# Expert products of eleven groups in three fp16 passes, an earlier load of the next tokens, and one lower half of E on the Pool engine

## The reference

```
x: (2, 2048, 256)            two sequences b, 2048 tokens, 256 channels, float32
x = x + layernorm(attention(layernorm(x)))          linear attention, no softmax
h = layernorm(x)
logits[b,m,n,p] = sum_d h[b,m,d] * phi[d,n,p]       n: 64 experts, p: 32 slots each
dispatch = softmax over b of logits                 2 sequences: a tanh of the difference
combine  = softmax over (n,p) of logits
slots[b,n,p,:] = sum_m h[b,m,:] * dispatch[b,m,n,p]
y[b,n,p,:] = slots[b,n,p,:] @ W[n] + bias[n]        W[n]: 256 x 256
out[b,m,:] = sum_{n,p} y[b,n,p,:] * combine[b,m,n,p]
x = x + layernorm(out)
```

## Time and profile before

| | us |
|---|---|
| median of 3 runs (654.32 to 654.46) | 654.41 |
| the profiled execution, whole | 654.63 |
| its span in the trace | 652.4 |
| PE busy | 630.5 (97%) |
| DVE busy | 437.7 (67%) |
| ACT busy | 367.3 (56%) |
| POOL busy | 237.5 (36%) |
| fp32 expert products in the block stage, L1606, PE busy | 23.2 |

### The profile page before, as it was taken

The page is one execution under the profiler, slowest core; times in us unless marked ns, Lnnn a source line. Parts: engine busy times, 40 slices in busy tenths (PEclk is TensorE's granted clock), DMA queues, the critical chain, the costliest instruction groups (busy, mean ns, idle before and its releaser), DMA issues.

```text
span 652.4 us, 15309 instructions
## 1 busy us (share of the span) xinstructions
PE 630.5 (97%) x5353; PEld 395.8 (61%) x5353; DVE 437.7 (67%) x859; ACT 367.3 (56%) x712; POOL 237.5 (36%) x416
## 2 busy tenths in 40 slices
PE   8999999999999999999999987799999999999996
PEld 7898645445444444444444455577777777777775
DVE  4978898733333423234333588999999988888885
ACT  5666876742333323324345295777777777777773
POOL 5365887710000000000000052555555555555555
PEclk9999999999999999999999999999999999999999
DMA  8910032325544544454455521132222222222201
GB/s 270 400 61 1 9 70 49 66 61 154 137 133 127 137 133 128 133 133 118 104 161 132 155 74 65 41 127 92 91 92 90 89 88 88 88 88 88 88 16 34
DMA packets 70167, 68.72 MB, mean 105 GB/s; under 512 B 6258, under 2 KB 66675, under 8 KB 67827
## 3 DMA queue, kind: packets, MB, share of 16 engines
q1 hardware_dynamic: 67792, 66.09, 34.4%
q10 hardware_dynamic: 2338, 2.16, 0.9%
HBM read 43.32 MB, written 23.07 MB: 102 GB/s over the span
## 4 chain that ended last, share of the span: by engine, by line
PE 75%; DVE 10%; POOL 5%; ACT 5%; issue 4%; DMA 1%; POOLq 0%; SPq 0%; DVEq 0%; ACTq 0%
PE psL L1589 23%; PE psM L1576 11%; PE psL L1708 10%; PE psM L1726 7%; PE psM L1727 6%; PE psM L1730 6%; PE psM L1606 3%; POOL small L489 2%; PE psL L1474 2%; ACT r_xn L868 1%; DVE small L1278 1%; DVE r_xn L1297 1%; ACT r L868 1%; DMA xres<-in_x 1%; PE psM L1532 1%
## 5 line engine op out<-in xcount | busy, mean ns | idle before, releaser
L1589 PE MATMUL psL<-r,r_xn 128*128 128x512 f16 x768 | 176.4, 379 | 0.8 <-DVE r L1119 0.8
L1589 PEld LDWEIGHTS psL<-r,r_xn 128*128 128x128 f16 x768 | 73.3, 98 | 91.6 <-issue 6.8
L1117 DVE TENSOR_SCALAR r<-r 128x512 f16<-128x512 f32 x64 | 29.0, 453 | 96.3 <-ACT r L758 96.3
L1576 PE MATMUL psM<-phs,xx 128*128 128x512 f16 (+1 forms) x384 | 93.2, 379 | 0.0
L758 ACT ACTIVATE r<-psM,small 128x512 f32<-128x512 f32 x64 | 43.6, 682 | 75.9 <-PE psM L1576 75.1
L576 POOL MEMSET r_xn<- 128x16 f16 x1 | 0.2, 173 | 234.9 <-PE psL L1589 234.9
L1708 PE MATMUL psL<-phs,r 128*32 128x512 f16 x1344 | 75.1, 379 | 2.0 <-DMA r<-xx 1.5
L1576 PEld LDWEIGHTS psM<-phs,xx 128*128 128x128 f16 x384 | 37.3, 98 | 44.8 <-issue 0.7
L868 ACT ACTIVATE r<-psL,small 128x512 f32<-128x512 f32 x60 | 41.9, 776 | 31.3 <-DVE small L1305 22.0
L489 POOL TENSOR_TENSOR small<-small,epst 128x2 f32<-128x2 f32 (+3 forms) x75 | 56.9, 759 | 6.2
L1708 PEld LDWEIGHTS psL<-phs,r 128*32 128x32 f16 x1344 | 34.6, 97 | 38.3 <-issue 2.6
(11 more groups left out here) (208 smaller groups left out, 1292.7 us busy)
## 6 DMA issues: line engine op xcount, KB each, us to landing
logit_difference<-r SPq DMA_DIRECT2D x256, 64.0 KB, 1.8
xx<-logit_difference SPq DMA_DIRECT2D x16, 1024.0 KB, 5.2
r<-in_ffn_w SPq DMA_DIRECT2D x15, 1024.0 KB, 5.5
out<-r SPq DMA_DIRECT2D x32, 128.0 KB, 1.7
xres<-in_x SPq DMA_DIRECT2D x7, 512.0 KB, 11.0
r<-in_phi SPq DMA_DIRECT2D x1, 2048.0 KB, 18.1
expert_bias<-r ACTq DMA_DIRECT2D x1, 2048.0 KB, 20.0
r<-expert_bias SPq DMA_DIRECT2D x16, 128.0 KB, 2.2
```

The source lines that it names most:

```text
L1576: ins = mm(bk[j % 2][:, :].rearrange("p (q m) -> p q m", q=EP), xxT[:, 1, j, hx, k, :], phw[:, hp, k, :, bass.ds(nb, 1), :].rearrange("p q ...
L1589: ins = mm(psL[:, i * 512:(i + 1) * 512], x3n[:, b, j, hx, k * P:(k + 1) * P], thl[:, j % 2, hs, :], start=(j == 0 and hx + hs == 0), stop ...
```

## The change

- The products of groups 0 to 10 (all of blocks 1 and 2, three of block 3) go in three fp16 passes. ACT writes the high half of a block's slots (`split_slots_hi`, at j = 0) and of a group's scaled weights (`weight_hi`, at j = 1, 4, 8, 12), DVE the low halves (`split_slots_lo` at j = 1, `weight_lo` at j = 2, 5, 9, 13). DVE finds a power of two for the weights of a group: `weight_top` (j = 2, 6, 10, 14) reads all 2048 columns, `weight_scale16` (j = 3, 7, 11, 15) brings the maximum over partitions in 15 small instructions. The bias instruction undoes the scale.
- The product moves one tile later on PE: behind j = 2, 6, 10, 14 (13 in the last block); bias and `y_sum` move to j = 3, 7, 11, 15 (14 in the last block).
- The weight halves (`Wp`) lie in r_3, so the load of `Wx` moves into block 3; SP's loads of `Wt` wait for `W_split` and not for the product.
- `load_x1` of the combination loop no longer waits for the mask, so `load_d` is first behind it.
- `lo(0, 1, 0)` is made by POOL.

```
-                    if j % 4 == 2:
-                        sp.wait_ge(yp_done, (nb - 1) * TB + (q + 1))
+                    if j % 4 == 0:
+                        sp.wait_ge(y_out, (nb - 1) * TB + (q + 2))
+                        sp.dma_start(by[:, (q + 1) % 2], ...)
+                    if j % 4 == 2 and not (last and q == TB - 1):
+                        sp.wait_ge(W_split, (nb - 1) * TB + (q + 1))
                         sp.dma_start(Wt[:, q % 2], ...)
...
             def loads(j):
+                wait_apart(sp, l_done, 4 * j)
+                load_x1(j)
                 wait_apart(sp, m0_masked, j)
-                load_x1(j)
                 load_d(j)
...
             mean(1, 0)
+            pool.wait_ge(eh_ready[0], 3)
+            nc.gpsimd.tensor_tensor(eT0[:, 1, 0:8, :]..., ET0[:, 0:1024],
+                                    eT0[:, 0, 0:8, :]..., ALU.subtract).then_inc(el0_pool, 1)
             lo_second(1)
...
+            def split_slots_hi(nb):
+                act.wait_ge(slots_evac, nb * 4 + 4)
+                act.wait_ge(yp_done, (nb - 1) * TB)
+                copy(slots_half[0]..., slT...).then_inc(slots_hi, 1)
+            def weight_hi(nb, q):
+                act.wait_ge(W_scaled, (nb - 1) * TB + (q + 1))
+                act.wait_ge(yp_done, (nb - 1) * TB + q)
+                copy(Wp[:, 0]..., Wt[:, q % 2]..., scale=sW[:, q % 2:q % 2 + 1]).then_inc(W_hi, 1)
             def block_act(nb, last):
                 for j in range(NJ):
                     tanh(nb, j)
                     d_copy(nb, j)
-                    if j % 4 == 2:
+                    if j == 0:
+                        split_slots_hi(nb)
+                    if j in (1, 4, 8) or j == 12 and not last:
+                        weight_hi(nb, j // 4)
+                    if j in (3, 7, 11, 14 if last else 15):
                         y_sum(...)
...
+            def weight_top(nb, q):
+                dve.wait_ge(W_loaded[w], ...)
+                own.add(V.tensor_reduce(wmax, Wt[:, w]..., AX_X, ALU.max, apply_absolute_value=True))
+            def weight_scale16(w):
+                # each line below waits for the one before it
+                transpose(topT, wmax.broadcast_to([P, Q]))
+                tensor_reduce(wquad, topT, AX_X, ALU.max)
+                4 x tensor_copy(wgath[0:Q, q:q + 1], wquad[q * Q:(q + 1) * Q])
+                tensor_reduce(wtop[0:Q, 0:1], wgath[0:Q], AX_X, ALU.max)
+                4 x tensor_copy(wtop[q * Q:(q + 1) * Q, 1:2], wtop[0:Q, 0:1])
+                tensor_scalar(max 2^-100); tensor_scalar(and exponent); tensor_scalar(* 2^-13); reciprocal
+            def split_slots_lo(nb):
+                dve.wait_ge(slots_hi, nb)
+                V.tensor_tensor(slots_half[1]..., slT..., slots_half[0]..., ALU.subtract).then_inc(slots_lo, 1)
+            def weight_lo(nb, q):
+                dve.wait_ge(W_hi, (nb - 1) * TB + (q + 1))
+                V.scalar_tensor_tensor(Wp[:, 1]..., Wt[:, q % 2]..., sW[...], Wp[:, 0]...,
+                                       ALU.mult, ALU.subtract).then_inc(W_split, 1)
             def block_dve(nb, last):
                 for j in range(1, NJ):
                     split(nb, j)
-                    if j % 4 == 2:
-                        y_bias(...)
+                    if j == 1:
+                        split_slots_lo(nb)
+                    if j in (2, 5, 9) or j == 13 and not last:
+                        weight_lo(nb, q)
+                    if j % 4 == 2 and not (last and q >= 2):
+                        weight_top(nb + (q + 1) // TB, (q + 1) % TB)
+                    if j in (3, 7, 11, 14 if last else 15):
+                        y_bias(..., not (last and q == TB - 1))
+                        if not (last and q >= 2):
+                            weight_scale16((q + 1) % 2)
...
+                    pe.wait_ge(W_split, yb_ * TB + (q + 1))
+                    if q == 0:
+                        pe.wait_ge(slots_lo, yb_ + 1)
+                    for b in range(B):
+                        for k in range(K):
+                            for hs, hw in ((0, 0), (0, 1), (1, 0)):
+                                for n in range(EP):
+                                    ins = mm(bk[2 + q % 2][...], slots_half[hs][:, k, n * TB + q, b, :],
+                                             Wp[:, hw, n, k, :], ...)
...
-                    if j % 4 == 1:
+                    if j in (2, 6, 10, 13 if last else 14):
                         y_product(nb - 1, j // 4, last)
```

More of the change, by code:

```diff
@@ L288, in build @@
         yp_done, y_out, ymx_ready = sem("yp_done"), sem("y_out"), sem("ymx_ready")
+        W_scaled, W_hi, W_split = sem("W_scaled"), sem("W_hi"), sem("W_split")
+        slots_hi, slots_lo = sem("slots_hi"), sem("slots_lo")
         brow_done, brow_ready, b_stored = sem("brow_done"), sem("brow_ready"), sem("b_stored")
@@ L1156, in xd_lo @@
                                 ALU.subtract).then_inc(xdl_ready, 1)
+            def weight_top(nb, q):
+                w = q % 2
+                dve.wait_ge(W_loaded[w], (nb - 1) * (8 * TB) + (16 * (q // 2) + 16))
+                own.add(V.tensor_reduce(wmax, Wt[:, w].rearrange("p n k e -> p (n k e)"), AX_X, ALU.max,
+                                        apply_absolute_value=True))
+            def weight_scale16(w):
+                own.wait()
+                own.add(V.transpose(topT, wmax.broadcast_to([P, Q])))
+                own.wait()
+                own.add(V.tensor_reduce(wquad, topT, AX_X, ALU.max))
+                own.wait()
+                for q in range(EP):
+                    own.add(V.tensor_copy(wgath[0:Q, q:q + 1], wquad[q * Q:(q + 1) * Q]))
+                own.wait()
+                own.add(V.tensor_reduce(wtop[0:Q, 0:1], wgath[0:Q], AX_X, ALU.max))
+                own.wait()
+                for q in range(EP):
+                    own.add(V.tensor_copy(wtop[q * Q:(q + 1) * Q, 1:2], wtop[0:Q, 0:1]))
+                own.wait()
+                own.add(V.tensor_scalar(wmax, wtop[:, 1:2], 2.0 ** -100, None, ALU.max))
+                own.wait()
+                own.add(V.tensor_scalar(wmax.bitcast(I32), wmax.bitcast(I32), 0x7F800000, None, ALU.bitwise_and))
+                own.wait()
+                own.add(V.tensor_scalar(isW[:, w:w + 1], wmax, 2.0 ** -TOP_EXP, None, ALU.mult))
+                own.wait()
+                V.reciprocal(sW[:, w:w + 1], isW[:, w:w + 1]).then_inc(W_scaled, 1)
             add_x(0, 0); add_x(0, 1); residual(0, 0); stats_x2(0, 0); add_x(0, 2); residual(0, 1)
@@ L1217, in slots_out, with y_bias @@
                                     ALU.mult, ALU.add).then_inc(slots_evac, 1)
-            def y_bias(i, q, bank, rows, loaded, value):
+            def y_bias(i, q, bank, rows, loaded, value, scaled=False):
                 dve.wait_ge(yp_done, i + 1)
                 wait_apart(dve, loaded, value)
+                if scaled:
+                    V.scalar_tensor_tensor(yf[:, :, bass.ds(i, 1), :].rearrange("p b t c -> p b (t c)"),
+                                           bank.rearrange("p (b c) -> p b c", b=B), isW[:, q % 2:q % 2 + 1],
+                                           rows.unsqueeze(1).broadcast_to([P, B, C]), ALU.mult, ALU.add).then_inc(y_out, 1)
+                    return
                 V.tensor_tensor(yf[:, :, bass.ds(i, 1), :].rearrange("p b t c -> p b (t c)"),
@@ L1317, in comb_dve @@
                 add_max(j, 1)
-                if third:
-                    lo(0, j - 1, 0)
-                elif not first:
+                if not first and not third:
                     exp_bias(0, j, FOLD[1], m1_folded, m1_ready)
@@ L1332, in comb_dve @@
                 turn(1, j, 1)
-                turns(0, j)
+                turns(0, j, first, third)
                 turn(0, j, 0)
@@ L1730, in low, with lows_ready @@
                 return mm(acc, eT[b][:, 1, t, :], yh(b, t), start=False, stop=last)
-            def lows_ready(b, j, half, last):
+            def lows_ready(b, j, half, last, second):
                 if b:
@@ L1736, in lows_ready @@
                 elif half and last:
-                    pe.wait_ge(el_ready[0], NJ + 1)
+                    pe.wait_ge(el_ready[0], NJ)
+                elif half:
+                    pe.wait_ge(el_pool, j + 1)
+                elif second:
+                    pe.wait_ge(el0_pool, 1)
                 else:
-                    pe.wait_ge(el_pool if half else el_ready[0], j + 1)
+                    pe.wait_ge(el_ready[0], j)
             def first_combine(b):
@@ L1795, in combine @@
                     if t % 8 == 0:
-                        lows_ready(b, j, t // 8, not more)
+                        lows_ready(b, j, t // 8, not more, second)
                     ins = low(b, t, acc, t == NT - 1)
```

77 lines of the change are left out of this document (54 added, 23 removed).

## The result

The change makes the kernel slower by 18.8 us: 673.06 us (median of six, 670.88 to 675.22) against 654.26 (653.82 to 654.46), a ratio of 1.0285 [1.0262, 1.0309]. Forecast were 659.3 and a range of 654.8 to 664.5: the sign was right, the size was not. One execution of the kernel of experiment 9 ran at a mean granted clock of 0.85 and took 726.9 us; its ratio leaves that one out.

A forecast was written before the change was run, and what follows sets the result against it. PE was taken to bound the kernel, with no idle time in the block stage. Block stage +6.1 and start of the combination -1.2 gave +4.9 us on the median of 654.41: 659.3 us, range 654.8 to 664.5.

The forecast's parts named there:

- eleven products: On PE in the block stage: each fp16 product takes 1.53 us instead of 1.96, gaining 0.43 eleven times, 4.8 us.
- 1, 2: second tile of blocks 1, 2, 3: `split_slots_hi` waits for `slots_out` with tanh queued behind it on ACT; PE waits 1.6, 1.9 and 1.7 us.
- 2: first bank, twice: At the end of blocks 1 and 2 `weight_scale16` precedes `slots_out` on DVE; PE waits 0.8 us each time.
- 3: six middle tiles: Between products, bias, scale and split on DVE end just behind PE's arrival: 0.1 us each, six times, 0.7.
- 4: `top_fold`, tile 8, turn: Last block: PE waits 1.9 us at `top_fold`, 0.85 for tile 8 and 1.1 at `turn_x1`, behind ACT's queue.
- short waits that went: PE's short waits for the low half in the block stage of the kernel before fall away: 0.4 us gained.
- block stage: Sum for the block stage: stalls 11.35 us, less 0.4 of short waits and 4.8 of product gain, +6.1 us.
- 5: start of the combination: POOL's half and the earlier token load let PE start at 421.3 instead of 422.48: -1.2 us, ends 0 and -3.1.
- 6 further copies at 0.07: Price inside `weight_scale16` on DVE: six copies at 0.07 us beside nine dependent steps at 0.20, 2.2 us, taken as 2.06.
- Rival B: `weight_scale16` takes 2.8 us, paid at eight or nine places, +6.6 us on the forecast: 666 us; chance 0.09.
- rival C: Weight loads or issue don't keep up with 256 columns; product takes 2.7 us, 14 on the forecast: 673 us; chance 0.04.

The follow-up runs named there:

- experiment 9: Changed kernel with scale, weight and slots halves and `y_hi` reordered, and `lo(0, 1, 0)` back on DVE: 651.55 us, ratio 0.9952 to the kernel before.
- experiment 6: Changed kernel with the scale's eight one-column copies each reading and writing the same 32 partitions, maximum over partitions left out: 668.56 us in one run.
- experiment 7: Changed kernel with the scale's eight one-column copies as multiplications by 1.0: 673.09 us in one run.
- experiment 8: Changed kernel with each group of four copies keeping one source and one target strip, maximum over all partitions left out: 665.9 us in one run.
- experiment 1: Changed kernel with `lo(0, 1, 0)` back on DVE: 670.18 us, ratio 1.0231 to the kernel before.
- experiment 4: Changed kernel with a fixed weight scale, the maximum over partitions and its power of two left out, `weight_top` kept: 661.5 us, ratio 1.0103 to the kernel before.
- experiment 5: Changed kernel with the tokens' copy moved in front of `weight_hi(1)` in the last block at j = 4: 669.88 us, ratio 1.0233 to the kernel before.
- experiment 3: Kernel before with only the early load of tokens (`load_x1` not waiting for the mask): 654.34 us against 654.2, ratio 1.0001.
- experiment 2: Kernel before with only `lo(0, 1, 0)` moved to POOL: 657.18 us against 654.2, ratio 1.0051.

## Why the prediction was right in direction and wrong in size

A wait in PE's pace is the idle time in brackets plus 0.17, since a group of slots matmuls lasts 2.76 us but the next one may start after 2.59 (1.46 and 1.29 for those of a logit difference).

| step of the prediction | forecast | measured |
|---|---|---|
| eleven products | -4.8 | -4.8 |
| 1, 2: second tile of blocks 1, 2, 3 | 1.6, 1.9, 1.7 | 1.60, 1.84, 1.26 |
| 2: first bank, twice | 0.8 each | 1.82, 1.92 |
| 3: six middle tiles | 0.7 | 6.9 |
| 4: `top_fold`, tile 8, turn | 1.9, 0.85, 1.1 | 2.82, 0.97, 1.11 |
| the clock behind `top_fold` | - | 2.9 |
| short waits that went | -0.4 | -0.5 (three of 0.18) |
| block stage | +6.1 | +17.8 by these terms, 18.25 by the landmark |
| 5: start of the combination | -1.2 | +3.05 |

- **Right:** the price of each wide operation, the product, which queue each delay stands in, and which places have slack. That weight loads of the same rows hide under matmuls held for the new product as well: 48 loads in 1.43 us.
- **Wrong, the size of the scale (prices, cases 2 to 4).** The step that failed is "6 further copies at 0.07": that price came from two instructions on the same partitions, while the copies go from strip to strip. They take 0.67 a group (experiments 6 to 8), the scale 2.77. Together with 0.2 us more from product to bias this makes 0.9 us in a chain that had no slack left: 0.1 becomes about 1.1 at six places, 0.8 becomes 1.9 at two. Rival B named this size (2.8 us) and was given 0.09; for the scale it is what happened. That the measured time equals the 673 of rival C is chance: C needed a product of 2.7 us, and it took 1.43. "This is on the edge: each 0.1 us more in the scale costs 0.1 at eight or nine places" was right, and was a reason for more weight on B and for a wider range. The Trainium skill ("VectorE: DVE Perf Modes", Two Vector instructions with no wait between them) says that a Vector instruction is held until all earlier ones have finished if its input or output starts in another quadrant of 32 partitions than the last one did. Experiments 6 and 8 bear it out: the first copy of a group aside, 0.065 us apart where both strips stay, 0.17 where one changes.
- **Missing, the clock (2.9 us in the block stage).** No term or rival had it. In the block stage it fell in the three profiled kernels in which `top_fold` waits 2.65 to 2.7 us (the changed one, experiments 1 and 7), and in none in which it waits 2.3, 2.0, 1.7 us or not at all (experiments 6, 8, 4, 5), each read from one execution. That the wait brings the fall is thus likely here, not shown. At the start of the combination it falls in nearly all of these kernels, at different places; in experiment 3's it falls at 398 us, where no wait of PE just before was over 1 us. So a long wait isn't needed for it, and what brings it about there isn't settled. It also differs between executions: of the changed kernel's six, the three with a mean clock of 0.992 took 673.0 to 675.2 us, the three with 0.995 took 670.9 to 673.2.
- **Wrong, case 5, in its sign.** "The half goes to POOL, ... long done when PE comes" was right of POOL and left out DVE, whose two scalings beside it grew from 0.75 to 2.7 and 2.6 us. Experiments 1 and 2 price it at 2.9 and 3.0 us, of which the profiled executions put about 1.6 down to the lower clock behind the wait. The Trainium skill ("GPSIMD Engine Reference", Specifications) lists the memory ports as shared with VectorE, with contention where a Vector instruction runs in a 2-port mode or has two inputs in SBUF; the trace agrees in that the fp16 scalings stretch; whether they run in such a mode, no run shows. The prediction left that rule out. The gain of 1.2 us from the earlier load failed as well: a gain at one wait of PE isn't a gain in the end where DVE is next (experiment 3).

Against the median of the changed kernel the forecast was 13.8 us short; in the profiled execution 16.1: 8.9 from the waits in the block stage, 2.9 from the clock in the block stage, 4.2 from case 5 (its own share of the clock included), and 0.1 of rest.

## What to carry to other kernels

Where a forecast puts the end of a chain on the very time at which the bound engine comes, price each small instruction in it by a row of the same kind, its partitions included, or widen the range by the number of places at which it recurs. Put a new chain behind the work that the bound engine waits for, not in front: the same instructions cost 15.5 us or gain 3.1 by order alone (experiments 1 and 9). Before giving work to GpSimd, look at what VectorE does at that moment, and call a wait that goes a gain only after the next tile has been checked for who is late then.

## What the runs showed of the hardware

- VectorE: four one-column copies of 32 partitions take 0.33 us on one strip, 0.67 where source or target changes strip each time, crossing or not, as copy or as multiplication.
- VectorE beside GpSimd: an fp16 scaling of 2048 columns takes 0.75 us alone, 2.6 to 2.7 when it starts together with, or during, a GpSimd subtraction of 1024 columns, and then ends 0.55 behind that. Maxima out of PSUM keep their time beside one.
- TensorE: 48 fp16 matmuls of 256 columns in four column strips, each with its own weights, start within 1.43 us, a group of four every 119 ns.
